# Unread 512-column matmul streams in two layers, and zero rows under a 48-row matmul, in a four-layer graph network

## The reference

```python
h = relu(layernorm(x))
x = x + (1 + eps) * h + segment_sum(relu(h[src] + edge_attr_32), dst)                # layer 0
h = relu(layernorm(x))
x = x + segment_sum(tensor_product_tanh(h[src], h[dst], edge_attr_3, edge_attr_10, W1, W2) * edge_weight, dst)   # layer 1, "tanh layer"
h = relu(layernorm(x))
x = x + gcn(h, row=src, col=dst)   # layer 2: norm * (sum of norm * h[dst] over edges of src, + self); norm = rsqrt(1 + out-degree)
h = relu(layernorm(x))
x = x + segment_sum(tensor_product(h[src], edge_attr_4, relu(edge_attr_8 @ fc_w1) @ fc_w2), dst) / sqrt(E / N)   # layer 3
```

## Time and profile before

| | |
|---|---|
| median of 3 runs | 23264.34 us (23223.69 to 23265.71) |
| the profiled execution | 23142.48 us |
| its span, first to last instruction | 23140.8 us |
| mean granted TensorE clock | 0.715 |
| PE busy | 14747.1 us (64%) |
| DVE busy | 12537.1 us (54%) |
| POOL busy | 10030.6 us (43%) |
| ACT busy | 7316.3 us (32%) |

### The profile page before, as it was taken

One profiled execution on the slowest core, in us unless ns is written; L12 is line 12 of the kernel. 1 busy time (PEld: TensorE's weight loads), 2 busy tenths in 40 slices (PEclk: granted clock), 3 DMA queues, 4 the chain that ended last, 5 costly groups with the idle time before them and its releaser, 6 DMA issues. The chain is left out here.

```text
span 23140.8 us, 410176 instructions
## 1 busy us (share of the span) xinstructions
PE 14747.1 (64%) x107469; PEld 10941.2 (47%) x108092; DVE 12537.1 (54%) x29165; ACT 7316.3 (32%) x22555; POOL 10030.6 (43%) x11407
## 2 busy tenths in 40 slices
PE   2444443433357777777777777777667777777777
PEld 1333333333345555555555555555445555555555
DVE  5455444554445555555555555555026666666666
ACT  1333333333323333333333333333002222222222
POOL 4455444454434444444444444443014555555554
PEclk7565655566667776777767777776888888888887
DMA  4666666666611111111111111110851111111111
GB/s 89 80 87 88 83 82 81 84 84 82 79 29 20 20 20 20 20 20 20 20 20 20 20 20 20 20 20 16 341 222 17 17 17 17 17 17 17 17 17 17
DMA packets 3048984, 1153.55 MB, mean 50 GB/s; under 512 B 2631873, under 2 KB 2993198, under 8 KB 3047249
## 3 DMA queue, kind: packets, MB, share of 16 engines
q1 hardware_dynamic: 2236554, 930.37, 19.8%
q0 software_dynamic: 312320, 178.52, 5.7%
q10 hardware_dynamic: 500000, 43.28, 2.3%
HBM read 767.02 MB, written 383.38 MB: 50 GB/s over the span
## 5 line engine op out<-in xcount | busy, mean ns | idle before, releaser
L1349 POOL DMA_INDIRECT w_rows<-table,w_idx x9375 | 8966.0, 956 | 6981.3 <-issue 2969.3
L1574 PE MATMUL w_p_w<-w_w,w_ht 128*128 128x256 f32 x12500 | 3743.4, 454 | 746.8 <-DVE w_prodv L1516 378.7
L1331 PE MATMUL w_p_deg<-w_hot_lo,w_hot_row 128*128 128x196 bf16 x6250 | 1956.2, 355 | 2574.5 <-issue 1210.7
L1574 PEld LDWEIGHTS w_p_w<-w_w,w_ht 128*128 128x128 f32 x12500 | 2762.7, 229 | 1717.7 <-issue 639.4
L1925 PE MATMUL w_p_xe<-w_xt,w_pick_b 128*128 128x128 bf16 x12500 | 1691.8, 279 | 1998.9 <-ACT w_xt L1911 1810.3
L1787 DVE TENSOR_TENSOR w_prod<-w_p_xe,w_he 128x512 f32<-128x512 f32 x3125 | 2123.7, 688 | 1012.7 <-PE w_p_xe L1925 999.1
L1734 POOL TENSOR_TENSOR w_dots<-w_v,w_unit 128x240 f32<-128x240 f32 x625 | 400.1, 640 | 4518.6 <-issue 3491.5
L1925 PEld LDWEIGHTS w_p_xe<-w_xt,w_pick_b 128*128 128x128 bf16 x12500 | 1032.9, 122 | 2762.5 <-ACT w_xt L1911 1665.2
L1145 ACT ACTIVATE w_dist<-row_iota,w_negrel 128x32 f32<-128x32 f32 x9375 | 2178.8, 313 | 442.6 <-issue 262.8
L1305 ACT CAST w_counts<-w_p_count 128x784 bf16<-128x784 f32 x1875 | 1237.1, 705 | 3410.6 <-remote 2107.1
L1331 PEld LDWEIGHTS w_p_deg<-w_hot_lo,w_hot_row 128*128 128x128 bf16 x6250 | 878.3, 141 | 2756.8 <-issue 1855.5
(11 more groups left out here) (209 smaller groups left out, 21512.5 us busy)
## 6 DMA issues: line engine op xcount, KB each, us to landing
counts<-w_counts SPq DMA_DIRECT2D x1250, 245.0 KB
d_rows<-counts SPq DMA_DIRECT2D x388, 784.0 KB
w_rows<-table,w_idx POOLq DMA_INDIRECT x9375
w_rel_row<-rel_row SPq DMA_DIRECT2D x625, 120.0 KB
w_edge<-e SPq DMA_DIRECT2D x625, 80.0 KB
w_idx<-src SPq DMA_DIRECT2D x1875, 2.5 KB
w_negrel<-negrel SPq DMA_DIRECT2D x1875, 2.5 KB
w_nodes<-split SPq DMA_DIRECT2D x1875, 2.0 KB
```

What stands on the lines that cost most here:

```text
L1331: nc.tensor.matmul(p_deg[:], hot_row[s2][:, b, :], hot_lo[s2][:, b, :], start=False, stop=False, skip_group_check=True)
L1349: pool.indirect_dma_start(out=rows[:, t, :], out_offset=None, in_=table[0:N, :], in_offset=bass.IndirectOffsetOnAxis(ap=idx[:, t:t + 1], a ...
L1574: last = nc.tensor.matmul(p_w[:, t * 256:(t + 1) * 256], ht[g.slot(2)][:, k, t * P:(t + 1) * P], w2[:, k, :], start=k == 0, stop=k == 1)
```

## The change

Matmuls whose results nobody reads are put into PE's order, and one tile gets more rows.

- Layer 0: a zero tile `still` of 128 by 512 is made once by POOL. Ahead of each of the three pieces, behind its wait, stand three matmuls of 512 bf16 columns into the bank that the piece will overwrite; behind `sum_window` stands a wait for ACT's copy of this group's first piece, and six more: 15 a group. They have zero weights and zero columns.
- Layer 1: three matmuls of 512 bf16 columns (identity by the constant `pick_b`) ahead of the hidden layer's matmul, and three ahead of the transposing ones, each into `p_he` and behind the waits that guard it: 6 a group.
- Layer 3: the attribute tile and the first weights are 128 rows deep in place of 48, the other 80 rows zero. The loads stay as they are.

```diff
@@ window_pass_0
+        still = sb("still", [P, 512], BF16)
...
             pool.memset(no_hot[:], 0.0).then_inc(zero_ready, 1)
+            pool.memset(still[:], 0.0).then_inc(zero_ready, 1)
...
+            def stream(bank, times):
+
+                for _ in range(times):
+                    nc.tensor.matmul(p_count[:, bank, :], no_hot[:, 0:P], still[:], start=True, stop=True)
+
+            pe.wait_ge(zero_ready, 2)
...
                         wait_count(pe, count_moved, g.times(len(PIECES), i + 1 - len(PIECES)))
+                        stream(b0, 3)
                         for b in range(2 * b0, 2 * b1):
...
                     w.sum_window(pe, g, msg[s2], msg_ready)
+                    pe.wait_ge(count_moved, g.times(len(PIECES), 1))
+                    stream(0, 6)
@@ window_pass_3
-        hidden = StackedEmbedding(nc, a, 3, sb, HID3)
+        hidden = StackedEmbedding(nc, a, 3, sb, HID3, P)
@@ window_pass_1
+            def stream(times):
+
+                for _ in range(times):
+                    nc.tensor.matmul(p_he[:, 0:512], ident_b[:], pick_b[:].rearrange("p i e -> p (i e)"), start=True, stop=True)
...
                     wg.product(pe, g)
                     free(pe, he_ready, g, 1)
                     free(pe, xt_ready, g, 2)
+                    stream(3)
                     for c0, c1 in ((0, 512), (512, GE)):
                         last = nc.tensor.matmul(p_he[:, c0:c1], hidden.weights[:], hidden.emb[s][:, c0:c1], start=True, stop=True)
...
                     pe.wait_ge(he_ready, g.times(1, 2 if at(1) else 1))
+                    stream(3)
                     for e in range(T):
                         last = nc.tensor.matmul(p_xt[:, e * P:(e + 1) * P], xs[g.slot(2)][:, e, :, :].rearrange("p s i -> p (s i)"),
                                                 ident_b[:], start=True, stop=True)
```

More of the change, by code:

```diff
@@ L1320, in _ @@
         def _(pe):
-            pe.wait_ge(zero_ready, 1)
+            def stream(bank, times):
+                for _ in range(times):
+                    nc.tensor.matmul(p_count[:, bank, :], no_hot[:, 0:P], still[:], start=True, stop=True)
+            pe.wait_ge(zero_ready, 2)
             nc.tensor.matmul(p_deg[:], no_hot[:, 0:P], no_hot[:], start=True, stop=False, skip_group_check=True)
```

## The result

| | before | after |
|---|---|---|
| median of 3 runs | 23264.34 us | 23596.39 us (23539.75 to 23614.36) |
| the profiled execution | 23142.48 us | 23539.75 us |
| its span | 23140.8 us | 23538.0 us |
| mean granted TensorE clock | 0.715 | 0.785 |

The ratio is 1.0143, with a 95% interval of 1.0111 to 1.0175: the change makes the kernel 1.4% slower. The forecast was 23,890 us. The direction and the range held; the shares of the layers did not.

The account below looks back on a forecast made before the run. Layer 1 was taken as bound by PE completions held during gathers, then by slow PE. 440 + 190 + 0 = +630 us on 23,142, plus 122 for a median: 23,890 us; own range 23,500 to 24,300, 8 in 10 22,600 to 24,700.

Parts of the forecast that it names:

- Completions are held while the gathers run: Layer 1: PE's completions are held back during POOL's gathers and let go about when the last has landed.
- Layer 1, +440 us: Layer 1's six streams push later PE steps back, most short groups turn long: +0.7 us a group, bounds -1,440 to +1,940 us.
- the short form: Layer 1 group whose copy of L2002's result slips through during the gathers: 9.4 + 5.2 = 14.6 us.
- If all did: 16.3 - 15.38 = +0.92 us: Layer 1: the cost a group if every group took the 16.3 us form, against the mean of 15.38 us.
- the long form: Layer 1 group whose copy of L2002's result is held to the gathers' end: 16.3 us, 46% of groups.
- L2002 by all six ... Fewer copies then slip through: Layer 1: all six streams delay L2002 by about 1.9 us, into the midst of the gathers, so more copies are held.
- completions ahead of L2002 are held too: Layer 1's upper bound: DVE's three products and a `contract` product remain after the release, +3.1 us a group.
- Layer 0, +190 us: Layer 0's fifteen streams: pieces end 0.5 us later, 0.3 us a group counted, bounds -190 to +1,060 us.
- the doubled clock pays for the streams and brings nothing beyond: Layer 0, one-hot to last piece: nine streams and 20 matmuls at full clock take 3.7 us, against 3.2 us now.
- Layer 3, 0: Layer 3's 80 zero rows cost nothing and a slightly higher clock brings nothing: 0 us, bounds -1,920 to +100 us.
- the second part: Layer 1, from the table sum to POOL's next start: 6.85 or 5.18 us, PE's and slow, at clock 0.50.
- the clock comes up where it matters: Rival: layer 1's streams carry PE at 2.4 GHz into the second part, -0.8 to -2.3 us a group; chance 0.28.

Follow-up runs that it names:

- e4: Changed kernel with all streams cut to 32 rows by 32 weight columns, a `nop` ahead of each set, no added layer 3 rows: 24886.57 us, ratio 1.0715.
- e12: Kernel before plus six layer 1 streams ahead of the transposing matmuls and five ahead of each layer 0 piece, chip D: 22769.14 us, ratio 0.9895.
- e3: Changed kernel without layer 0's last six streams and their wait, and without layer 1's three ahead of the hidden matmul: 23135.93 us, ratio 0.9939.
- e1: Kernel before plus only layer 0's 15 streams, chip A: 22912.01 us, ratio 0.9861.
- e9: The changed kernel itself, run again on chip C: 23178.71 us, ratio 1.0097 to the kernel before.
- e10: Kernel before plus twelve layer 1 streams at the end of PE's step; layer 0 three ahead of each piece, twelve last; chip C: 21863.92 us, ratio 0.9527.
- e2: Changed kernel without layer 0's nine streams ahead of pieces, layer 1's three ahead of the transposing matmuls, and layer 3's rows: 23838.21 us, ratio 1.0242.
- e11: Kernel before plus layer 0's streams as changed and sixteen layer 1 streams at the end of PE's step, chip D: 21493.67 us, ratio 0.9342.
- the bridge: Layer 1 streams at the end of PE's step, behind the window matmul, replacing the change's six: twelve in e10, sixteen in e11; ratios 0.9527 and 0.9342.

## Why the prediction was right or wrong

The total came out inside the forecast's range partly by luck: layer 1 lost 291 us more than I had counted, and layer 0 was 552 us better.

**Completions are held while the gathers run.** Right for layer 1 on chips A, C and D. Its opposite fits: where nothing is held, the same program takes 15,763 us. The prediction took it as a trait of the kernel; it depends on the machine, and by `e4`'s layer 0 on the program as well. By the Trainium skill ("SBUF — State Buffer", "SBUF: two separate sides") a DMA cannot slow a compute op. The matmuls themselves agree with it, 0.48 us for the five transposing ones in the earlier trace rows and on chip B; what comes late on the others is their completion, which the section does not speak of.

**Layer 1, +440 us against +731.** The mechanism was right in its form: groups turn from the short form to the long one, which 44% had before (the prediction worked out 46%). "If all did: 16.3 - 15.38 = +0.92 us" is what happened, in all 513 groups, and the long form became another 0.2 to 0.4 us longer (16.24 to 16.42 and 16.60). The step that failed is what turns them, "L2002 by all six ... Fewer copies then slip through": I put it on L2002's start and expected a part of the groups to escape. L2002 moved by 1.2 us and not by 1.9. `e12` moves it as far and loses 0.16 us; `e3` moves it by 0.6 and loses 0.08. It is the streams ahead of the hidden matmul that turn every group, by moving that matmul's end by 1.2 us and with it every completion behind it. I had "completions ahead of L2002 are held too" as the upper bound at +3.1 us. It is the rule in 83 of 121 groups, and its price was wrong: about 0.2 us, since a longer first part is made up in the second (table sum at 11.1 us and 5.5 us behind it, against 9.5 and 7.0). The first three streams also run cold, at 0.42 us each.

**Layer 0, +190 us against -362.** The step that failed: "the doubled clock pays for the streams and brings nothing beyond". The clock came as forecast (0.87). The last piece's matmul ends 6.8 us behind the end of DVE's one-hot against 4.3 before, +2.5 us and not the +0.5 I counted, and yet groups are shorter on average. (The upper bound also has a slip: half of 7.0 - 3.2 is 1.9 us, not 1.7. Nothing hangs on it.) So the path from the one-hot to the pieces, on which the term was built, does not set the mean. What changed is the spread: from one start of POOL's gathers to the next, the median rose from 7.4 to 8.2 us, while groups over 11 us fell from 24% (43% of the time) to 14% (23%). Copies of ACT that start over 5 us behind the end of their piece fell from 29% to 20%. POOL's wait for its index load, L1349 and L1359, 2000 to 4000 us, before and after:

```profile
POOL w_rows L1349 <- DMA w_idx<-src: 704.5, 98, 13.3
```

```profile
POOL w_rows L1359 <- DMA w_idx<-src: 599.2, 146, 12.5
```

That is 3.40 us a group (207 groups) against 2.71 (221), -0.69, more often but shorter; it covers the gain of 0.58. SP issues these loads in order behind its wait for ACT's copies, so late pieces do starve POOL. Across the kernels on holding chips the period mostly falls with the clock, and the place of the streams matters less:

| streams a group | clock | us a group |
|---|---|---|
| none | 0.60 | 9.56 |
| 6 last | 0.73 | 9.48 |
| 9 ahead | 0.78 | 9.28 |
| 15 ahead | 0.87 | 8.95 |
| 9 ahead, 6 last | 0.87 | 8.86 to 8.99 |
| 9 ahead, 12 last | 0.94 | 9.08 |
| 15 narrow | 0.50 | 10.99 |

The row at 0.94 breaks the order, though: 9.08 us, where the same chip gave 8.88 at 0.87. The last row has the half clock and a full PE together, and cannot tell the two apart. How a faster PE makes the long groups rarer is argued, not shown: shorter pieces are more often complete between two bursts of gathers. I have no run that separates this from the clock, and it stays open.

**Layer 3, 0 against +26 us.** Right. With 128 rows 9.38 (`e3`) and without 9.38 (`e1`) on chip A; 9.19 (`e9`) and 9.18 (`e10`) on chip C. `e2`, without the rows, had 9.50 in one trace, so 0.1 us is chance here.

**The clock.** 0.87, 0.71 and 0.50 in the second part, against 0.85, 0.72 and 0.50 in the prediction. The reason given, that the idle stretch ahead of the slow part remains, is borne out by `e10` and `e11`: once streams fill it, the second part has 0.78 and 0.89.

**The rival "the clock comes up where it matters"** was priced at -0.8 to -2.3 us a group. As a mechanism it is real: the bridge of `e10` and `e11` brings layer 1 to 13.93 and 13.57 us, 1.4 and 1.7 us below 15.30 (from another chip, so within 0.2 us). The change's streams stand where PE is busy already, the bridge's where it idles.

## What to carry to other kernels

Streams that are to hold TensorE's clock belong in PE's idle stretch ahead of the slow part, behind everything of the group that others wait for; ahead of a matmul whose result is awaited they are a delay, and here the delay of an early step, which moves every completion behind it, decided, not that of the last step alone. Before such a change is trusted, run it on more than one chip: the bridge gave -6.6% where completions are held, and twelve streams of it, with more in layer 0, +7.0% where they are not. Of the kernels here `e11_bridge16` is the fastest on the first kind and the kernel before on the second; `e11` itself was not run there.

## What the hardware showed that was not expected

- The kernel before takes 15,763 us on one chip and 22,950 to 23,265 on three others. On those three ACT idles for up to 6.1 us in layer 1 (`e12`, 9000 to 11000 us) for completions of PE while indirect DMAs run; on the one they are seen within 0.1 us of the matmul's end. Within one execution on chip A, `e4`, they are held in layer 1 and not in layer 0.
- Held completions of layer 1 come out in PE's order, in each of 533 and 486 groups before and after.
- With streams of 32 rows by 32 weight columns (and a `nop` ahead of each set) PE was busy for 5,400 of 5,400 us and granted 0.50 throughout; with 128 by 128 the granted clock was 0.87.
- The clock is a result of the waits as much as a cause: layer 1 without any change has 0.70 where completions are held, and 1.00 where they are not (there with one stream a group).
